# Two layers of attention and mixture on one core: second-layer query and key units turned late on GpSimd, and small work reordered

## The reference, cut to what matters

```python
x = layernorm(x + attention_0(x))      # 16 heads of 16 channels, causal, biases
x = layernorm(x + mixture_0(x))        # 8 experts, two per token, and a shared one
x = layernorm(x + attention_1(x))      # 16 heads, not causal, rotary q and k, no biases
x = layernorm(x + mixture_1(x))        # 4 experts of 256 slots each; a token takes its two best
```

```python
q1r = q1 * cos + rotate_half(q1) * sin     # first half of a head's channels; the rest is left alone
att = softmax(einsum('bhqd,bhkd->bhqk', q, k) / sqrt(HD))
```

```python
sel_p, sel_idx = top_k(score, capacity)
tok = flat_x[sel_idx]
out = out.at[sel_idx].add(gelu(tok @ W1[i]) @ W2[i] * p)
```

## Time and profile before

| what | us |
|---|---|
| runs, median (lowest to highest) | 631.4 (627.77 to 632.14) |
| profiled execution, time | 630.31 |
| its span | 628.5 |
| attention 1: first unit's matmul to first score tile | 297.53 to 320.09 |
| attention 1: first transposed scores, last exponential | 342.27, 504.13 |
| norm of attention 1, first statistics to end of the last split | 508.92 to 521.68 |
| mixture 1: begin of its block to the first expert's first matmul | 522.33 to 548.46 |
| PE, DVE, ACT, POOL busy | 587.4, 483.3, 367.9, 186.5 |

### The profile page before, as it was taken

How to read it: one execution, slowest core, us unless ns; L and a number is a source line. 1 busy time by engine, 2 the same in 40 slices (tenths; PEclk the granted TensorE clock), 3 DMA queues, 4 the chain that set the end, 5 groups by cost and what they waited for, 6 DMA issues and landing times. The chain is left out here.

```text
span 628.5 us, 13108 instructions
## 1 busy us (share of the span) xinstructions
PE 587.4 (93%) x4908; PEld 376.4 (60%) x4908; DVE 483.3 (77%) x919; ACT 367.9 (59%) x712; POOL 186.5 (30%) x352
## 2 busy tenths in 40 slices
PE   2989999998999999997998999999999998899995
PEld 1754545554777888895864333333333375799995
DVE  5587988985857767547788899999999668969635
ACT  3426877887455433353122788988888836156652
POOL 4303566666023222213330012212121100336720
PEclk9967999999999999998997899999999998979998
DMA  4424756642231111000170234435341144305532
GB/s 179 61 41 51 153 87 99 93 72 81 60 126 50 52 50 50 25 1 1 67 102 1 36 52 65 60 59 78 50 73 52 46 141 133 135 12 174 168 86 67
DMA packets 23321, 46.95 MB, mean 75 GB/s; under 512 B 10160, under 2 KB 15136, under 8 KB 20960
## 3 DMA queue, kind: packets, MB, share of 16 engines
q1 hardware_dynamic: 18976, 38.98, 30.3%
q0 software_dynamic: 4288, 7.20, 4.0%
HBM read 25.22 MB, written 7.83 MB: 53 GB/s over the span
## 5 line engine op out<-in xcount | busy, mean ns | idle before, releaser
L521 ACT ACTIVATE probs<-ps 128x512 f32<-128x512 f32 x448 | 222.3, 554 | 54.8 <-PE ps L420 42.0
L392 PE MATMUL ps<-stacks 62*128 62x512 f32 x448 | 159.6, 440 | 4.4 <-DVE row_max L630 1.9
L630 DVE TENSOR_REDUCE row_max<-ps 128x1 f32<-128x1024 f32 x128 | 154.6, 1218 | 6.9 <-PE ps L392 4.8
L420 PE MATMUL ps<-stacks 64*128 64x512 f32 x448 | 157.7, 433 | 1.9 <-DMA stacks<-max_rows 0.9
L435 PE MATMUL ps<-probs,v_ones 128*32 128x256 f32 (+7 forms) x2048 | 135.9, 349 | 3.8 <-ACT probs L521 1.7
L420 PEld LDWEIGHTS ps<-stacks 64*128 64x128 f32 x448 | 71.6, 190 | 80.0 <-ACT probs L521 59.6
L627 DVE CUSTOM_DVE_ANT_0 y_sums<-ps,wide_mask 128x1024 f32<-128x1024 f32 (+7 forms) x128 | 91.6, 751 | 21.8 <-PE ps L392 10.3
L435 PEld LDWEIGHTS ps<-probs,v_ones 128*32 128x32 f32 x2048 | 41.8, 109 | 77.0 <-ACT probs L521 48.1
L392 PEld LDWEIGHTS ps<-stacks 62*128 62x128 f32 x448 | 72.4, 196 | 15.5 <-DVE row_max L630 5.9
L986 POOL TENSOR_TENSOR w_chunk_l_m<-y_sums,w_chunk_h_m 128x512 fp32r<-128x512 f32 (+1 forms) x24 | 24.2, 1030 | 90.7 <-ACT w_chunk_h_m L1059 83.4
L587 POOL TENSOR_SCALAR_AFFINE_SELECT probs<-probs 128x128 f32<-128x128 f32 x128 | 38.1, 310 | 41.0 <-ACT probs L521 40.0
(11 more groups left out here) (220 smaller groups left out, 1165.0 us busy)
## 6 DMA issues: line engine op xcount, KB each, us to landing
stacks<-part_rows SPq DMA_DIRECT2D x32, 256.0 KB, 4.7
y_sums<-in_w_experts SPq DMA_DIRECT2D x8, 1024.0 KB, 5.1
y_sums<-in_w_chunks SPq DMA_DIRECT2D x12, 384.0 KB, 3.0
stacks<-part_rows SPq DMA_DIRECT2D x32, 128.0 KB, 5.2
head_sums<-sums POOLq DMA_DIRECT2D x28, 128.0 KB, 2.2
stacks<-max_rows SPq DMA_DIRECT2D x128, 2.0 KB
y_sums<-head_sums POOLq DMA_DIRECT2D x28, 64.0 KB, 3.9
y_sums<-sum_rows SPq DMA_DIRECT2D x28, 64.0 KB, 2.3
```

The lines of the kernel that those rows point to most:

```text
L392: mm = pe.matmul(scores_bank(s, a, b), stack("q_stack", h, slice(0, TOP))[:, qt * P:(qt + 1) * P], stack("k_stack", h, slice(0, TOP))[:, a ...
L420: pe.matmul(bank(at % 3, 0, b - a), stack("k_stack", h, slice(0, SIDE))[:, kt * P:(kt + 1) * P], stack("q_stack", h, slice(0, SIDE))[:, a: ...
L521: act.activation(probs[:, t % 4, a:b], bank(at % 3, 0, b - a), ACT.Exp).then_inc(exp_done, 1)
L630: dve.tensor_reduce(row_max[:, h % 2, qt:qt + 1], scores_bank(s, 0, end), AX.X, ALU.max).then_inc(scores_free, 1)
```

## The change

**Attention 1.** Units 4 to 7 are taken out of the start. PE does units 0 to 3, then V for all eight tiles (`EARLY_V` is 8), then the lead. Each of the 16 lead tiles is followed by one `late_products`, half of one of the two products of a unit of 4 to 7. ACT copies each finished product out of PSUM to `late_raw` (`late_to_sbuf`), POOL does both multiplications and the sum (`turn_late`), ACT the high part (`late_high`), POOL the low part (`late_low`). The high part of unit 7 stands on ACT behind the exponentials of step 7. For units 0 to 3 the low part is now on DVE. `split_max` of heads 0 and 1 stands among POOL's late work, that of head 2 behind all of it. The tables have memory of their own, and `late_raw` uses memory in which sums of heads are put later. ACT does not wait for `low_ready[1]` any more; SP still does, ahead of the stacks of head 4.

**Exponential table.** One exponential of one column (`first_exp`) is put ahead of the loop and, in mixture 1, ahead of the token splits, so that the table load stands there.

**Norms.** In both attention norms the reciprocal of tiles 0 to 3 comes right after the statistics of tile 3. In all norms ACT normalises tiles 4 and 5, DVE 6 and 7.

**Mixture 1.** The token splits on DVE (L1548) move from between the router's copies to behind the weights; the exponential of `TopTwo` moves ahead of the weight splits on ACT; the low part of the first expert's W1, 2048 columns, moves from DVE (L1539) to POOL; eight unread matmuls instead of twelve; and the comparison for expert 1 is interrupted for `split_slots` and `take_slots` after three tiles instead of five.

```diff
-EARLY_V = (5, 0)
+EARLY_V = (5, 8)
...
+        tables = sb("tables", [P, 2, T]) if rope else None
+        late_raw = mem["y_sums"][:, 1:3, :, :].rearrange("p n k t -> p (n k t)").rearrange("p (u r c) -> p u r c", u=4, r=2)
...
+        norm = NormStage(nc, ctx, mem, f"a{layer}", first_bank=3, source=lambda t: out_bank(t), invert_after=3)
...
+        def late_bank(u, r):
+
+            return bank(((0, 1), (2, 7))[u % 2][r])
...
+            def late_products(u, r, k):
+
+                t, m, n = units[u]
+                name, cols, w = t + "p" if r else t, slice(n * HALF, (n + 1) * HALF), slice(k * D + m * P, k * D + (m + 1) * P)
+                if k == 0:
+                    if u == 4:
+                        pe.wait_ge(v_out, NT - 1 + r)
+                    elif u == 5:
+                        pe.wait_ge(unit_out, 4)
+                    else:
+                        pe.wait_ge(late_out, 2 * (u - 6) + r + 1)
+                mm = product(pe, late_bank(u, r), (mem["wa_h"][:, w_at[name], w], mem["wa_l"][:, w_at[name], w]),
+                             (mem["xt_h"][:, k, cols], mem["xt_l"][:, k, cols]), k == 0, k == KD - 1)
+                if k == KD - 1:
+                    mm.then_inc(late_ready, 1)
+
...
                 if t < 2:
-                    pe.wait_ge(unit_out, 5)
+                    pe.wait_ge(unit_out, 1 if rope else 5)
...
                 if at >= 3:
                     pe.wait_ge(exp_done, at - 2)
+                elif rope:
+                    pe.wait_ge(late_out, at + 5)
...
                 if kt == 0 and h:
                     pe.wait_ge(sums_out, h)
+                elif kt == 0 and rope:
+                    pe.wait_ge(late_out, 8)
...
-            for u in range(8):
+            for u in range(4 if rope else 8):
                 unit(u)
...
             for s in range(LEAD):
                 if s < 2:
-                    pe.wait_ge(unit_out, s + 7)
+                    pe.wait_ge(unit_out, s + (3 if rope else 7))
                 scores(s, 0)
                 scores(s, 1)
+                if rope:
+                    late_products(4 + s // 4, s % 4 // 2, s % 2)
                 if s + EARLY_V[layer] < NT:
                     project_v(s + EARLY_V[layer])
             pe.wait_ge(v_out, NT)
...
                     v_to_sbuf(s + EARLY_V[layer])
+            act.activation(first_exp[:, :], mem["eps"][:, :], ACT.Exp)
+
+            def late_to_sbuf(u):
+                for r in range(2):
+                    act.wait_ge(late_ready, 2 * (u - 4) + r + 1)
+                    act.activation(late_raw[:, u - 4, r, :], late_bank(u, r), ACT.Copy, scale=HD ** -0.5 if units[u][0] == "q" else 1.0
+                                   ).then_inc(late_out, 1)
+
+            def late_high(u):
+                act.wait_ge(late_turned, u - 3)
+                act.activation(part_rows[:, part(u, False), u % 2 * HALF:(u % 2 + 1) * HALF], late_raw[:, u - 4, 0, :], ACT.Copy
+                               ).then_inc(high_ready, 1)
+
+            if rope:
+                late_to_sbuf(4)
+                late_to_sbuf(5)
+                late_high(4)
+                late_to_sbuf(6)
+                late_high(5)
+                late_to_sbuf(7)
+                late_high(6)
 
             def exps(t):
                 for n, (a, b) in enumerate(st_pieces(t)):
...
 
             act.wait_ge(low_ready[0], 4)
-            act.wait_ge(low_ready[1], 4)
+            if causal:
+                act.wait_ge(low_ready[1], 4)
             for t in range(H * NT):
                 exps(t)
...
-            split_max(0)
+            def turn_late(u):
+
+                cols, (a, b) = slice(u % 2 * HALF, (u % 2 + 1) * HALF), (late_raw[:, u - 4, r, :] for r in range(2))
+                if u < 6:
+                    pool.wait_ge(tables_in[u % 2], 16)
+                pool.wait_ge(late_out, 2 * (u - 4) + 1)
+                pool.tensor_tensor(a, a, tables[:, 0, cols], ALU.mult).then_inc(late_step, 1)
+                pool.wait_ge(late_out, 2 * (u - 4) + 2)
+                pool.tensor_tensor(b, b, tables[:, 1, cols], ALU.mult).then_inc(late_step, 1)
+                pool.wait_ge(late_step, 2 * (u - 4) + 2)
+                pool.tensor_tensor(a, a, b, ALU.add).then_inc(late_turned, 1)
+
+            def late_low(u):
+
+                high, low = [part_rows[:, part(u, l), u % 2 * HALF:(u % 2 + 1) * HALF] for l in (False, True)]
+                pool.wait_ge(high_ready, u + 1)
+                pool.tensor_tensor(low, late_raw[:, u - 4, 0, :], high.bitcast(F32), ALU.subtract).then_inc(low_ready[1], 1)
+
+            if rope:
+                turn_late(4)
+                split_max(0)
+                turn_late(5)
+                late_low(4)
+                turn_late(6)
+                split_max(1)
+                late_low(5)
+                turn_late(7)
+                late_low(6)
+                late_low(7)
+            else:
+                for u in range(4, 8):
+                    unit_low(u)
+                split_max(0)
             for t in range(H * NT):
...
-                if kt == 0 and h + 1 < H:
+                if kt == 0 and h >= rope and h + 1 < H:
                     split_max(h + 1)
                 if causal:
...
 
-            for u in range(8):
+            for u in range(4 if rope else 8):
                 unit_to_flat(u)
-                if not rope and 1 <= u <= 4:
+                if 1 <= u <= 4:
                     unit_low(u - 1)
+            if rope:
+                unit_low(3)
 
...
+        if t == self.invert_after:
             self.invert(dve, 0)
 
     def invert(self, dve, g):
...
+                                 op0=ALU.mult, op1=ALU.mult).then_inc(self.shift_ready, 1)
         if g:
-            for t in range(4, NT):
+            for t in range(6, NT):
                 dve.tensor_scalar(self.mem["x"][:, t, :], self.source(t), self.mv[:, t, 0:1], self.rstd[:, t:t + 1],
-                                  ALU.subtract, ALU.mult).then_inc(self.normed[1], 1)
-            return
-        dve.scalar_tensor_tensor(out=self.shift[:, tiles], in0=self.mv[:, tiles, 0], scalar=-1.0, in1=self.rstd[:, tiles],
-                                 op0=ALU.mult, op1=ALU.mult).then_inc(self.shift_ready, 1)
+                                  ALU.subtract, ALU.mult).then_inc(self.normed[2], 1)
 
     def scalar(self, act):
         x = self.mem["x"]
...
-                    act.activation(x[:, t, :], self.source(t), ACT.Identity, bias=self.shift[:, t:t + 1], scale=self.rstd[:, t:t + 1]
-                                   ).then_inc(self.normed[0], 1)
+            act.wait_ge(self.shift_ready, g + 1)
+            for t in range(4 * g, 6 if g else 4):
+                act.activation(x[:, t, :], self.source(t), ACT.Identity, bias=self.shift[:, t:t + 1], scale=self.rstd[:, t:t + 1]
+                               ).then_inc(self.normed[g], 1)
         if not self.last:
             for n in range(4):
                 k, g = n % 2, n // 2
...
 
+            pool.wait_ge(w_high[0], 1)
+            pool.wait_ge(row_ready, 1)
...
             router.scalar(act, r_raw)
+            act.activation(first_exp[:, :], mem["eps"][:, :], ACT.Exp)
             for n in range(2):
                 act.activation(x_h[:, 4 * n:4 * n + 4, :], x[:, 4 * n:4 * n + 4, :], ACT.Copy).then_inc(xh_ready, 1)
             act.activation(ident[:, :], consts[:, C_ID:C_ID + P], ACT.Copy).then_inc(preset, 1)
+            top.scalar(act)
             split_weights(0, 0)
             split_weights(0, 1)
-            top.scalar(act)
             for n in range(2):
                 act.wait_ge(turned_ready, n + 1)
                 act.activation(part_row[:, n * HALF:(n + 1) * HALF], bank(XG + n)[0:2 * E1, :], ACT.Copy).then_inc(part_row_out, 1)
...
-            keep_warm(12)
+            keep_warm(8)
...
             compare(0, 0, NT)
             assign(0)
-            compare(1, 0, 5)
+            compare(1, 0, 3)
             split_slots(0)
             take_slots(0)
-            compare(1, 5, NT)
+            compare(1, 3, NT)
             for e in range(E1):
                 if e == 0:
```

37 lines of the change are left out of this document (19 added, 18 removed).

## The result

The kernel after took 628.07 us in the median of 20 runs (624.61 to 653.89), the kernel before 631.3 (626.41 to 635.38, 20 runs). The ratio is 0.995, with a 95% interval of 0.9928 to 0.9973: faster by 3.2 us, at most 4.5 and at least 1.7. The forecast was 626.0, with 621.0 to 631.0 as range and "within 1%" as the likeliest class; both held. The forecast drop was 5.4 us and the measured one 3.2, so it was the range that held, and not the sum. Medians here are over all runs, while ratios leave out disturbed ones, of which the kernel after had three in 20 (648 to 654 us) and the kernel before none, so that the means over all 20 runs, 631.3 and 631.0, show no gain.

A forecast was written before the change was run, and what follows sets the result against it. PE was busy 93% of the span, and PE and DVE both full in attention 1's loop. Attention 1 -0.8, norms -1.6, router -1.1, first expert -1.2 and -0.7 made -5.4: 624.9 profiled, 626.0 as median, range 621.0 to 631.0.

The forecast's parts named there:

- step 5: Attention 1's loop: with PE kept full, the first five steps take 6.2 us for 9.2, so step 5 comes 1.9 sooner.
- the jam behind unit 7: Attention 1's loop: head 2's maxima split waits behind unit 7's high and low parts, giving back 1.1 us of 1.9.
- PE, two tiles ahead, runs into it: Attention 1's loop: PE, two tiles ahead of DVE, is also held by DVE's wait of 1.1 us.
- Norms: Attention 1's norm 0.85 us sooner, attention 0's 0.6, the last 0.15: together -1.6, between 0 and -2.3.
- Router: Mixture 1: the comparison starts 1.1 us sooner, between 0 and -1.7, held by ACT's copies behind the weight splits.
- First expert: Mixture 1: PE's wait of 1.21 us for the token split goes (-1.2), and the clock gives -0.7, between 0 and -5.0.
- Rival B: Mixture 1: the clock holds in the first expert, 4 of the 5.0 us come back instead of 0.7; 622.7, chance 0.22.
- Rival C: Attention 1: PE's new waits of 1.9 and 2.0 us bring the clock down, costing +2; 628.0, chance 0.20.
- D: Attention 1's lead: the same clock fall lasts 14 us, +7.0, so the kernel is slower at 633.0; chance 0.07.
- PE has no wait in the lead: Attention 1's lead: the argument against D; PE had waits in the earlier low stretch of 14 us.
- Rival E: Mixture 1: POOL, busy until 543.2, holds DVE's one-hots of the first expert, +3.0; 629.0, chance 0.10.
- The table load: Attention 1: the load of 1.28 us leaves ACT's loop, counted as even against two copies; the skill's 2.66 would give 1.4 more.

The follow-up runs named there:

- two_waits_moved: Kernel after with unit 7's high part behind step 5's exponentials and a POOL subtraction for expert 1 waiting for DVE's 2048-column one: 632.71 us, ratio 1.0042.
- attention_alone: Kernel before with only the attention edits (late units, V ahead of the lead, early exponential): 628.92 us, ratio 0.9984.
- norms_alone: Kernel before with only the edits of the norms: 628.61 us, ratio 1.0004.
- mixture_alone: Kernel before with only the edits of mixture 1: 629.84 us, ratio 1.0001.
- after_again: Kernel after unchanged, run again beside others on the same chip: 628.79 us, ratio 0.9960 against the kernel before.
- after_waits_filled: Kernel after with five and three unread 512-column matmuls in PE's waits ahead of the first score tile: 647.21 us, median of 6 runs.
- twelve_fillers: Kernel after with twelve unread matmuls for eight ahead of the router's transposes: 636.39 us, ratio 0.9954 against the kernel before.
- filled_router: Kernel after with 13 unread matmuls for 8 ahead of the router's transposes and 5 for 2 behind them: 631.88 us, ratio 0.9993.
- filled_lead: Kernel before with two unread 512-column matmuls behind each of the last eight score tiles of attention 1's lead: 630.53 us, ratio 1.0025.

## Why the prediction was right, and where not

**Right, with its sizes:** the first tile (21.2 us after the first unit, predicted 318.4 - 297.53 = 20.9), the tile spacing (1.55 for 1.56), the loop's begin 1.2 later than before for 1.1, the clock at 1.00 through the lead, step 5 earlier by 1.8 for 1.9, and the jam behind unit 7.

**The jam was mis-sized:** 0.36 for 1.1. DVE waited 0.62, not 1.1: POOL split 58.04 us after the first unit where the prediction had 58.4, and DVE was done 0.2 later than it said. Of the 0.62 only 0.36 reached PE; the step that failed is "PE, two tiles ahead, runs into it", at its full length. two_waits_moved measured the jam again, by taking it away: 0.35. Attention 1 gave 1.5 for 0.8.

**Norms:** 0.6 and 0.6 in the profiled execution for 0.85 and 0.6, and the second not in every trace, so 0.9 to 1.2 for 1.6; the last 0.15 was not there.

**Router:** 1.29 between the two traces for 1.1. But the old code takes 10.88, not 11.44, where the low stretch does not meet its twelve fillers (attention_alone, norms_alone): 0.7 is the edit's and 0.55 the clock's. The comparison waits for ACT's copies behind the weight splits, as predicted (1.04 of PE's wait).

**First expert: the failed step.** The prediction has "-1.2, all of that wait" and "-0.7 of clock", in all 3.0 with the router. Measured by mixture_alone: nothing, give or take 2 us (ratio 1.0001). The wait did go: 6.2 for 7.5. At a high clock the first expert then takes 9.99 for 9.3, since PE meets the last comparisons, which the prediction named without a price: the 36 one-column rank matmuls span 1.7 us for 0.9 in norms_alone, and 0.7 is given back. The rest is the clock, and not as a saving: its low stretch now falls 9 to 11 us behind `pick`, into the comparisons (after, mixture_alone, after_again, after_waits_filled), and costs 1.8 to 2.7 there. The mean from `pick` to the end is 104.6 us over six traces of the old mixture (102.3 to 106.1) and 104.2 over these four of the new (103.5 to 105.2). No trace has the new code with the clock high from `pick` to the second expert, so what its order alone is worth stays open. Rival B (the clock holds in the first expert) is right by its letter in after, and gained 3.5 there, but 2.7 of it was paid 10 us earlier; no rival of mine had the clock falling in a new place of mixture 1. The second expert gives back 1.2 more of what a high clock gains in the first (9.4 for 8.25), in the old code as in the new, and the prediction had no term for this either.

**Rival C and D** said that PE's new waits would bring the clock down in the lead. The waits came (1.79 and 0.54), the clock fell between them, and it cost nothing. A far longer fall than D's 14 us exists (47.8), once with the waits as they are (twelve_fillers) and once with them filled. "PE has no wait in the lead", which the prediction held against D, did not prevent it: PE was busy for all of the 39.8 us from the fall to the loop.

**Rival E** (POOL beside DVE) is true as a mechanism, with 1.8 us on the one-hots in filled_router, and hidden in after. The prediction took it from the Trainium skill that only the small addition is caught. But the Trainium skill (SBUF — State Buffer, Who interferes with whom) names `tensor_scalar`, the form of the one-hots, among those that can enter a two-port mode, so it does not leave them out. They were slowed, and they followed each other 0.26 us apart for 256 columns when alone (2.19 for eight); whether that is a two-port mode no run here shows. The small addition ahead of them took 1.02 us in after, for 0.17 in before, and in mixture_alone one of the one-hots was held also (0.90, 2.73 for the eight).

**The table load:** 1.28 us, and the first exponential follows it in filled_lead within 0.02 us. The drain of the Trainium skill (ScalarE: Activation LUTs, What ACT_TABLE_LOAD costs) does not show here. What the load costs beyond its 1.28 us is in part argued: in filled_lead the clock fell within PE's wait for it.

So by stages the change is worth 1.5 + 0.9 to 1.2 + 0 to 0.5, that is 2.4 to 3.2, where the forecast had 0.8 + 1.6 + 3.0; the runs have 3.2, with 1.7 to 4.5 as interval. That the forecast of 626.0 lay 2.1 below the result and inside its range is in part luck: attention 1 gave 0.7 more than its term, mixture 1 2.5 to 3.0 less.

## What to carry to other kernels

Before moving real work into a stretch with a low clock, try the two cheapest things, unread matmuls in the idle share of PE and the table load moved out of the wait; here they gave 3.1 us of the stage where the move gave 1.5. Compare executions by the stages' lengths with their granted clock beside, since a low stretch in untouched code moved the total by more than the whole change. And a gain read off a stretch at half clock must be asked where the low clock goes next.

## What the chip showed that I had not expected

- A busy PE did not mean a high clock: in two traces with late units it was at 0.50 for 47.8 us, though PE had no wait from the fall to the loop, once with its waits ahead of the tiles filled and once without.
- DVE's 2048-column subtraction took 2.28 us alone and 4.03 with a POOL subtraction running for the first 1.87 of it; eight one-hots of 256 columns 2.19 and 3.96. DVE's comparison, with one input in PSUM, took 1.28 both with POOL's 2048-column subtraction beside it and without.
- A filler of 512 columns cost 0.33 us between score tiles, for 0.235 a matmul in the units, so fillers must be priced from the place where they stand.
